# Moving the block epilogue of a selective-scan kernel from behind the sixth scan to behind the fourth

## Chip, cores and metric

The kernel runs on all 8 cores of one Trainium2 chip. Each core takes two of the 16 sequences; the cores exchange nothing. The metric is the device time in microseconds of the slowest core.

## What is computed

One layer: a layer norm of x, a state-space branch and a structured (tensor-train) linear branch, both added to x.

```python
x_and_res = x @ in_proj_w.T + in_proj_b
x_in = silu(x_and_res[..., :d_model]);  res = x_and_res[..., d_model:]
ssm = x_in @ x_proj_w.T + x_proj_b          # dlt_raw (16), Bm (1024), Cm (1024)
delta = clip(softplus(dlt_raw @ dt_proj_w.T + dt_proj_b), 1e-05, 0.1)
def step(h, inp):                           # h: d_model x 16 states
    dt, Bt, Ct, xt = inp
    dA = clip(exp(A * dt[..., None]), 1e-06, 1.0)
    h = clip(h * dA + (Bt * dt * xt)[..., None], -100.0, 100.0)
    y = sum(h, axis=-1) * Ct + D_param * xt
    return (h, y)
return y * silu(res) @ out_proj_w.T + out_proj_b
```

x is 16 x 2048 x 1024 in float32. The last line is y times silu(res), projected by the output weights.

## The kernel before

**Tiles.** A core's two sequences are cut into 8 chunks of 512 time steps (4 chunks each). The 1024 channels are 8 blocks of 128 partitions, and each channel has 16 states, so the recurrence of one chunk is 8 x 16 = 128 scans of 128 x 512. I write s(k,n) for the scan of block k, state n.

**The scan pipeline.** ACT computes `da` = exp(delta * A) for each scan (`emit_da`, L895) into a ring of 8 buffers; it may write the buffer of scan G only when scan G-8 is done. DVE runs the scan itself (L835) into `h_buf`, a ring of 8 slices (`HR = 8`); it may write slice G only when PE has consumed slice G-8. PE adds the 16 states of a block by a multiplication with the identity, accumulating in a PSUM bank (`emit_sigma`, L557; banks pS and pS2 alternate by block). I call this the sum of s(k,n). After every fourth scan a small DVE instruction (L845, "clip") saves the carries. When the 16 sums of block k are in, DVE's epilogue of that block (`emit_epi`) multiplies the bank by C (L806, writes y_s) and adds D*x (L814, writes y2_s); then POOL multiplies y2_s by silu(res) (L454) into the tile that the output projection reads.

```python
wt(v, "t", ("summ", cS * 128 + kk * NST + NST - 1))   # L806 waits: 16th sum
wt(v, "g", ("attn", cS * 8 + kk - 1))                 # L814 waits: POOL's L454 of the block before
if n == 5 and k >= 1:                                 # L851: where the epilogue of block k-1 stands
```

The epilogue of block k-1 thus stands in DVE's program inside block k. That of block 7 stands behind the last scan of the chunk. In chunk 0 those of blocks 0 and 1 stand together inside block 2.

**Three chunks at once.** While chunk c is scanned, the other engines also write out chunk c-1 (output projection and structured branch L585 and L590, evacuation L927, transposes L603, L936, residual addition on POOL L473 with its loads `xr_t`) and then prepare chunk c+1: layer norm of four tiles t = 0 to 3 (statistics on ACT L948 and L952, small mean and variance arithmetic on POOL L435, L437, L440, L443, L446, rstd on ACT L957 and L960, normalising on ACT, transposes on PE L624, evacuation L988 and L998), the input projection (16 groups, L647, evacuated with silu, L1020), the x projection (L682; L1033, L1039, L1045) and delta (L699, L1058, L1066, L1070).

**What sets the order.** Every engine runs one static list. PE's and ACT's lists are interleaved by a table `BNDS` of estimated times: before each group, `pump` and `apump` place the sums and `da` that the table finds due. For chunks 1 to 6 this puts the sums up to s(2,14) ahead of the fourth transpose group of the layer norm (t = 3), and the sums of s(2,15), s(3,0), s(3,1), s(3,2) right behind it, ahead of the input projection. POOL's list is sorted by due times too; in chunk 0 it holds `emit_w4`, which loads the structured weights with 16 DMAs of small pieces (L407), ahead of the first multiplication L454. ACT's exp/ln and its silu need different activation tables, so each switch costs an ACT_TABLE_LOAD.

Of the kernel before, what the change touches and what calls it, by code (L numbers as in the profile page):

```python
# [44 lines left out]
def build_core(M_in, M_out):  # L45
# [28 lines left out]
    with es:  # L74
# [79 lines left out]
        def mark(key, chain):  # L154
            M_out[key] = chain.n
# [5 lines left out]
        def wt(eng, chain_id, key):  # L161
            val = M_in.get(key, 0)
            if val > 0:
                wt_stat[0] += 1
                hk = (id(eng), chain_id)
                if wait_hi.get(hk, 0) >= val:
                    wt_stat[1] += 1
                    return
                wait_hi[hk] = val
                eng.wait_ge(CH[chain_id].sem, val)  # L170
# [31 lines left out]
        def h_sl(gn):  # L202
            r = gn % HR
            return h_buf[:, r * TC:(r + 1) * TC]
# [6 lines left out]
        def c_(tile, i):  # L211
            return tile[:, i:i + 1]
# [505 lines left out]
        def _(v):  # L718
            v_hi = [0]

            def vsw(val):
                if val > v_hi[0]:
                    v_hi[0] = val
                    v.wait_ge(VCH.sem, val)
# [35 lines left out]
            def emit_ffev4(q):  # L760
                for gidx in range(4 * q, 4 * q + 4):
                    half, m = divmod(gidx, 8)
                    if gidx == 8:
                        v.wait_ge(DS["pd2"], 16)
                    wt(v, "t", ("ffmm", gidx))
                    bank = [pO1, pO2][gidx % 2]
                    w4v = xr_t[0][:, :].bitcast(F16)
                    VCH(v.tensor_copy(w4v[:, m * 256:(m + 1) * 256],
                                      bank[:, 0:256]))
                    mark(("ffev", gidx), VCH)  # L770
                    if gidx in (7, 15):
                        mark(("w4ev", gidx // 8), VCH)

            def emit_wneg():
                v.wait_ge(DS["pd2"], 32 + 16 * 16)
                for kk in range(4):
                    VCH(v.tensor_scalar(w_ffn[4 + kk][:, 0:512],
                                        w_ffn[4 + kk][:, 0:512], -1.0, None,
                                        op0=ALU.mult))
                mark(("wneg",), VCH)  # L780
# [18 lines left out]
            def emit_epi(cS, kk, P):  # L799
                if cS == 0 and kk == 0:  # L800
                    wt(v, "t", ("ffmm", 15))
                wt(v, "t", ("summ", cS * 128 + kk * NST + NST - 1))
                sbank = [pS, pS2][kk % 2]
                if ep2_n[0] > 0:
                    vsw(ep2_n[0])
                ey = VCH(v.tensor_mul(y_s[:, :], sbank[:, :],  # L806
                                      Cf[P][kk][:, :]))
                mark(("epiy", cS * 8 + kk), VCH)
                if kk >= 1:
                    wt(v, "g", ("attn", cS * 8 + kk - 1))  # L810
                elif cS >= 1:
                    wt(v, "g", ("attn", (cS - 1) * 8 + 7))
                vsw(ey)
                ep2_n[0] = VCH(v.scalar_tensor_tensor(  # L814
                    y2_s[:, :], xin[P][kk][:, :], c_(d_cols, kk), y_s[:, :],
                    op0=ALU.mult, op1=ALU.add))
                mark(("epi2", cS * 8 + kk), VCH)

            for cS in range(nch):
                P = cS % 2  # L820
                b, ci = divmod(cS, NCHB)
                for k in range(DCH):
                    for n in range(NST):
                        gn = k * NST + n
                        G = cS * 128 + gn
                        wt(v, "a", ("da", G))
                        if G - HR >= 0:
                            wt(v, "t", ("summ", G - HR))
                            cn = clip_n.get((G - HR) // 4, 0)
                            if cn > 0:  # L830
                                vsw(cn)
                        if gn == 0 and last_clip[0] > 0:
                            vsw(last_clip[0])
                        init = 0.0 if ci == 0 else c_(carry[k], n)
                        s_n = VCH(v.tensor_tensor_scan(  # L835
                            h_sl(gn), da_r[gn % DAR][:, :], Bu[P][k][:, :],
                            init, op0=ALU.mult, op1=ALU.add))
                        mark(("scan", G), VCH)
                        if n % 4 == 3:
                            vsw(s_n)  # L840
                            base = (gn - 3) % HR
                            src = bass.AP(h_buf, base * TC + TC - 1,
                                          [[HR * TC, 128], [TC, 4]])
                            clip_n[(cS * 128 + gn - 3) // 4] = VCH(
                                v.tensor_scalar(carry[k][:, n - 3:n + 1], src,  # L845
                                                100.0, -100.0, op0=ALU.min,
                                                op1=ALU.max))
                        if cS == 0 and gn == 23:
                            for q_ in range(4):
                                emit_ffev4(q_)  # L850
                        if n == 5 and k >= 1:  # L851
                            if cS == 0 and k == 1:
                                pass
                            elif cS == 0 and k == 2:
                                emit_epi(0, 0, P)
                                emit_epi(0, 1, P)
                            else:
                                emit_epi(cS, k - 1, P)
                        if cS == 0 and gn == 96:
                            emit_wneg()  # L860
                emit_epi(cS, DCH - 1, P)
                last_clip[0] = clip_n.get((cS * 128 + 124) // 4, 0)
# [252 lines left out]
```

## Time and profile before

| | us |
|---|---|
| median of 2 runs | 2245.6 (2241.46 to 2249.75) |
| the profiled execution | 2249.66 |
| span of its slowest core (core 2) | 2247.9 |
| spans of the eight cores | 2225.2 to 2247.9 |
| mean granted TensorE clock, core 2 | 0.756 |
| first scan starts, core 2 | 301.7 |
| chain that ended last | PE 37%, DVE 21%, issue 12%, ACT 11%, DMA 9%, POOL 7% |

The span runs from the first to the last instruction of the slowest core; the device time is 1.8 us more. All rows below are of core 2 of the profiled execution, in us from the start of its span. In the timeline views the columns are start, duration, engine, line, operation, out<-in, shape and the number of merged instructions; in brackets stands how long the engine was idle before, and what ended that.

### The profile page before, as it was taken

What the parts mean: (1) busy time and instruction counts of PE and PEld (TensorE: products, weight loads), DVE (VectorE), ACT (ScalarE), POOL (GpSimd) and SP (SyncE); (2) the same over time, 40 slices, a digit from 0 to 9 for tenths busy, and PEclk for the clock granted to TensorE, in tenths of its full rate; (3) what the DMA queues carried; (4) which work ended last, traced back from release to release, by engine and by line L of the source; (5) the groups of instructions that cost most, each with busy time, mean ns of one, the idle gap of its engine ahead of it and who ended that gap; (6) DMA issues with size and microseconds to landing.
All of it is one profiled execution on the core that took longest, in us unless ns stands there. A gap on an engine that the chain in (4) does not pass through costs nothing.

```text
span 2247.9 us, 21779 instructions; the slowest of 8 cores (2225.2 to 2247.9 us)
## 1 busy us (share of the span) xinstructions
PE 1240.8 (55%) x5104; PEld 511.8 (23%) x5104; DVE 1612.4 (72%) x1600; ACT 1253.0 (56%) x1873; POOL 614.6 (27%) x506
## 2 busy tenths in 40 slices
PE   1222846265464857385729572867277627755444
PEld 1111313021121313131314131323132213322012
DVE  1332044069985999499949995899589967999980
ACT  0004465476456955695559655965586558745531
POOL 0000041318122161307131713171317131523001
PEclk9999976676585968696859785978598758866557
DMA  5672322630011301240024003310332022202001
GB/s 142 190 183 71 114 75 36 66 63 25 1 66 66 113 19 44 77 126 19 29 85 124 27 10 103 100 52 10 103 90 61 10 103 81 71 1 75 1 10 65
DMA packets 106882, 151.92 MB, mean 68 GB/s; under 512 B 53232, under 2 KB 53240, under 8 KB 106760
## 3 DMA queue, kind: packets, MB, share of 16 engines
q1 hardware_dynamic: 97128, 120.10, 18.3%
q0 software_dynamic: 6176, 19.93, 4.1%
q10 hardware_dynamic: 3456, 10.52, 1.5%
q8 instruction: 46, 0.75, 0.1%
q14 instruction: 76, 0.62, 0.1%
HBM read 124.26 MB, written 26.25 MB: 67 GB/s over the span
## 4 chain that ended last, share of the span: by engine, by line
PE 37%; DVE 21%; issue 12%; ACT 11%; DMA 9%; POOL 7%; SPq 1%; DVEq 0%; ACTq 0%; POOLq 0%
DVE h_buf L835 19%; PE pM L682 7%; PE pS L557 7%; PE pO L585 5%; DMA xr_t<-x 5%; PE pM L647 5%; PE pO L590 4%; PE pO L647 4%; POOL out_tm L473 3%; ACT da L895 3%; PE pO L682 2%; ACT rx L952 1%; ACT rx L948 1%; POOL wf L407 1%; PE pT L519 1%
## 5 line engine op out<-in xcount | busy, mean ns | idle before, releaser
L835 DVE TENSOR_TENSOR_SCAN h_buf<-da,cr,Bu 128x512 f16<-128x512 f16 x768 | 1053.3, 1427 | 114.1 <-PE pS L557 112.2
L895 ACT ACTIVATE da<-dlt,ac 128x512 f16<-128x512 f16 x1024 | 695.2, 715 | 292.3 <-DVE h_buf L835 290.4
L557 PE MATMUL pS<-h_buf,eye 128*128 128x512 f16 x1024 | 422.0, 475 | 332.4 <-DVE h_buf L835 322.6
L835 DVE TENSOR_TENSOR_SCAN h_buf<-da,Bu 128x512 f16<-128x512 f16 x256 | 331.8, 1351 | 157.5 <-ACT da L895 114.3
L454 POOL TENSOR_TENSOR Bu<-y_s,sres 128x512 f16<-128x512 f32 x64 | 126.2, 1973 | 763.4 <-DVE y_s L814 763.4
L557 PEld LDWEIGHTS pS<-h_buf,eye 128*128 128x128 f16 x1024 | 108.4, 107 | 569.9 <-issue 508.2
L682 PE MATMUL pM<-xin,rx 128*128 128x512 f16 (+1 forms) x832 | 197.2, 382 | 26.0 <-ACT sres L1020 22.0
L473 POOL TENSOR_TENSOR out_tm<-otm,xr_t 128x1024 f32<-128x1024 f16 x32 | 75.6, 2362 | 230.9 <-ACT otm L936 121.7
L647 PE MATMUL pM<-xnf,rin 128*128 128x512 f16 x512 | 133.1, 409 | 3.8 <-ACT sres L1020 2.5
L585 PE MATMUL pO<-Bu,wo 128*128 128x512 f16 x512 | 132.5, 406 | 3.1 <-POOL Bu L454 3.1
L647 PE MATMUL pO<-xnf,rin 128*128 128x512 f16 x512 | 123.6, 387 | 7.7 <-DMA rin<-wt_in 7.7
L590 PE MATMUL pO<-xnf,wf 128*128 128x512 f16 x512 | 123.2, 384 | 0.0
L519 PE MATMUL pT<-eye,rx 128*128 128x128 f16 x320 | 40.5, 307 | 140.6 <-DVE rx L732 140.6
L682 PEld LDWEIGHTS pM<-xin,rx 128*128 128x128 f16 (+1 forms) x832 | 79.7, 97 | 128.8 <-issue 36.6
L435 POOL TENSOR_SCALAR mcol<-sumx 128x1 f32<-128x1 f32 x32 | 12.6, 393 | 350.0 <-ACT rx L952 350.0
L876 ACT ACT_TABLE_LOAD x1 | 1.3, 1283 | 187.7 <-DVE rx L732 187.7
L624 PE MATMUL pT<-eye,xn_tm 128*128 128x128 f16 x128 | 16.2, 306 | 156.1 <-ACT xn_tm L967 94.2
L814 DVE SCALAR_TENSOR_TENSOR y_s<-xin,d_cols,y_s 128x512 f32<-128x512 f16 x64 | 56.2, 878 | 63.7 <-POOL Bu L454 57.1
L936 ACT ACTIVATE otm<-pTo 128x1024 f16<-128x1024 f16 x32 | 32.6, 1019 | 116.6 <-POOL out_tm L473 115.7
L927 ACT ACTIVATE ao<-pO,bcomb 128x512 f16<-128x512 f32 x64 | 43.8, 684 | 90.2 <-PE pO L590 90.1
L845 DVE TENSOR_SCALAR cr<-h_buf 128x4 f16<-128x4 f16 x256 | 72.6, 283 | 27.2
L624 PE MATMUL pT<-eye,xin 128*128 128x128 f16 x128 | 16.2, 307 | 136.6 <-ACT xnf L988 136.6
(83 smaller groups left out, 1539.3 us busy)
## 6 DMA issues: line engine op xcount, KB each, us to landing
rin<-wt_in SPq DMA_DIRECT2D x128, 256.0 KB, 2.8
rx<-wt_x SPq DMA_DIRECT2D x128, 256.0 KB, 2.7
x_t<-x SPq DMA_DIRECT2D x32, 512.0 KB, 4.6
xr_t<-x POOLq DMA_DIRECT2D x32, 512.0 KB, 5.0
y<-out_tm SPq DMA_DIRECT2D x32, 512.0 KB, 3.6
wt_in<-rin SPq DMA_DIRECT2D x16, 256.0 KB, 2.8
wt_x<-rin SPq DMA_DIRECT2D x16, 224.0 KB, 3.6
x_t<-w_in ACTq DMA_DIRECT2D x4, 512.0 KB, 3.9
```

The costliest lines, as they stand in the source:

```text
L454: GCH(gp.tensor_mul(Bu[P][k][:, :], y2_s[:, :], sres[P][k][:, :]))
L473: GCH(gp.tensor_add(out_tm[g % 2][:, :], otm16[:, :], xr_t[g % 2][:, :]))
L519: TCH(te.transpose(pT1[:, k * 128:(k + 1) * 128], wst16[j % 2][:, k * 128:(k + 1) * 128], eye16[:, :]))
L557: TCH(te.matmul(sbank[:, :], eye16[:, :], h_sl(gn), start=(n == 0), stop=(n == NST - 1)))
L585: TCH(te.matmul(bank[:, :], w_out[k][:, m * 128:(m + 1) * 128], Bu[P][k][:, :], start=(k == 0), stop=False))
L590: TCH(te.matmul(bank[:, :], w_ffn[k][:, m * 128:(m + 1) * 128], xn_f[P][:, k * TC:(k + 1) * TC], start=False, stop=(k == DCH - 1)))
L647: TCH(te.matmul(bank[:, :], rin[slot][:, k * 128:(k + 1) * 128], xn_f[P][:, k * TC:(k + 1) * TC], start=(k == 0), stop=(k == DCH - 1)))
L682: TCH(te.matmul(out_ap, rx[slot][:, k * ncols:(k + 1) * ncols], xin[P][k][:, :], start=(k == 0), stop=(k == DCH - 1)))
L814: ep2_n[0] = VCH(v.scalar_tensor_tensor(y2_s[:, :], xin[P][kk][:, :], c_(d_cols, kk), y_s[:, :], op0=ALU.mult, op1=ALU.add))
L835: s_n = VCH(v.tensor_tensor_scan(h_sl(gn), da_r[gn % DAR][:, :], Bu[P][k][:, :], init, op0=ALU.mult, op1=ALU.add))
L845: v.tensor_scalar(carry[k][:, n - 3:n + 1], src, 100.0, -100.0, op0=ALU.min, op1=ALU.max))
L895: ACH(sc.activation(da_r[gn % DAR][:, :], dlt[Ps][k][:, :], AF.Exp, scale=c_(a_cols[k], n)))
```

## The change

One number changes: the epilogue of block k-1 is issued when n == 3 instead of n == 5.

```diff
-                        if n == 5 and k >= 1:
+                        if n == 3 and k >= 1:
                             if cS == 0 and k == 1:
                                 pass
                             elif cS == 0 and k == 2:
                                 emit_epi(0, 0, P)
                                 emit_epi(0, 1, P)
                             else:
                                 emit_epi(cS, k - 1, P)
```

No other engine's list changes: PE, ACT, POOL and SP run the same instructions in the same order. On DVE 56 of the 64 epilogues move ahead of two scans, at 55 places (blocks 1 to 7 of 8 chunks; chunk 0 has none in block 1 and two in block 2).

The first place is DVE in chunk 0, inside block 2 (Bu_2 is the scan input of block 2, Cf_0 and Cf_1 the C tiles of blocks 0 and 1):

```order
 L835 SCALAR_TENSOR_TENSOR h_buf<-da,Bu_2 128x512 x4
 L845 TENSOR_SCALAR cr<-h_buf 128x4
-L835 SCALAR_TENSOR_TENSOR h_buf<-da,Bu_2 128x512 x2
 L806 TENSOR_TENSOR y_s<-pS,Cf_0 128x512
 L814 SCALAR_TENSOR_TENSOR y_s<-xin_0,d_cols,y_s 128x512
 L806 TENSOR_TENSOR y_s<-pS,Cf_1 128x512
 L814 SCALAR_TENSOR_TENSOR y_s<-xin_1,d_cols,y_s 128x512
-L835 SCALAR_TENSOR_TENSOR h_buf<-da,Bu_2 128x512 x2
-L845 TENSOR_SCALAR cr<-h_buf 128x4
 L835 SCALAR_TENSOR_TENSOR h_buf<-da,Bu_2 128x512 x4
```

The scans s(2,4) and s(2,5) stood ahead of the two epilogues and now stand behind them.

The second place is DVE in chunk 1, inside block 3 (Cf_2 belongs to block 2). Before:

```order
L845 TENSOR_SCALAR cr<-h_buf 128x4
L835 SCALAR_TENSOR_TENSOR h_buf<-da,cr,Bu_3 128x512 x2
L806 TENSOR_TENSOR y_s<-pS,Cf_2 128x512
L814 SCALAR_TENSOR_TENSOR y_s<-xin_2,d_cols,y_s 128x512
L835 SCALAR_TENSOR_TENSOR h_buf<-da,cr,Bu_3 128x512 x2
```

and of the changed kernel at the same place:

```order
L845 TENSOR_SCALAR cr<-h_buf 128x4
L806 TENSOR_TENSOR y_s<-pS,Cf_2 128x512
L814 SCALAR_TENSOR_TENSOR y_s<-xin_2,d_cols,y_s 128x512
L835 SCALAR_TENSOR_TENSOR h_buf<-da,cr,Bu_3 128x512 x4
L845 TENSOR_SCALAR cr<-h_buf 128x4
```

The scans s(3,4) and s(3,5) now stand behind the epilogue of block 2, in one row with s(3,6) and s(3,7).

## Rows read from the trace of the kernel before

**Rows 1.** The page: its first line and its busy times.
```profile
span 2247.9 us, 21779 instructions; the slowest of 8 cores (2225.2 to 2247.9 us)
PE 1240.8 (55%) x5104; PEld 511.8 (23%) x5104; DVE 1612.4 (72%) x1600; ACT 1253.0 (56%) x1873; POOL 614.6 (27%) x506
```
**Rows 2.** View of line L806: what ended DVE's idle time before it (us, times).
```profile
  PE pS L557: 54.2, 16
```
**Rows 3.** Timeline of DVE, chunk 1, from the layer norm to the epilogue of block 2.
```profile
680.47 4.33 DVE L835 TENSOR_TENSOR_SCAN h_buf<-da,cr,Bu 128x512 f16<-128x512 f16 x2 [10.62 <-PE pS L557]
...
707.47 2.46 DVE L835 TENSOR_TENSOR_SCAN h_buf<-da,cr,Bu 128x512 f16<-128x512 f16 x2
716.86 0.69 DVE L806 TENSOR_TENSOR y_s<-pS,Cf 128x512 f32<-128x512 f32 x1 [6.93 <-PE pS L557]
718.33 3.31 DVE L835 TENSOR_TENSOR_SCAN h_buf<-da,cr,Bu 128x512 f16<-128x512 f16 x2
```
**Rows 4.** DVE busy in the stretches behind block 2's epilogue, chunks 1 to 6.
```profile
717.00:839.00 122.00, 118.75 (x105) 0.81 0.24 70
...
sum 728.00, DVE 707.88; mean DVE 117.98
```
**Rows 5.** Timeline of PE, chunk 1: sums of s(2,15) and s(3,0) to s(3,2).
```profile
716.17 1.86 PE L557 MATMUL pS<-h_buf,eye 128*128 128x512 f16 x4 [1.37 <-ACT xnf L998]
```
**Rows 6.** Timeline of ACT, chunk 1, from the layer norm into the input projection.
```profile
710.01 0.29 ACT L957 ACTIVATE rstd<-vcol,eps_c 128x1 f32<-128x1 f32 x1 [2.85 <-POOL vcol L443]
...
721.73 0.72 ACT L895 ACTIVATE da<-dlt,ac 128x512 f16<-128x512 f16 x1 [1.31 <-DVE h_buf L835]
...
725.82 0.69 ACT L1020 ACTIVATE xin<-pO,bin_c 128x512 f16<-128x512 f32 x1 [0.80 <-PE pO L647]
727.98 0.69 ACT L1020 ACTIVATE xin<-pO,bin_c 128x512 f16<-128x512 f32 x1 [1.47 <-PE pO L647]
```
**Rows 7.** Timeline of POOL, chunk 1: residual additions, variance arithmetic of tiles 0 and 3.
```profile
653.50 2.72 POOL L473 TENSOR_TENSOR out_tm<-otm,xr_t 128x1024 f32<-128x1024 f16 x1 [12.64 <-ACT otm L936]
661.71 2.12 POOL L473 TENSOR_TENSOR out_tm<-otm,xr_t 128x1024 f32<-128x1024 f16 x1 [4.95 <-DMA xr_t<-x]
...
675.70 0.19 POOL L440 TENSOR_TENSOR nmr<-mcol 128x1 f32<-128x1 f32 x1
676.04 0.19 POOL L443 TENSOR_TENSOR vcol<-vcol,nmr 128x1 f32<-128x1 f32 x1
...
707.68 1.06 POOL L440 TENSOR_TENSOR nmr<-mcol 128x1 f32<-128x1 f32 x1
708.88 1.03 POOL L443 TENSOR_TENSOR vcol<-vcol,nmr 128x1 f32<-128x1 f32 x1
```
**Rows 8.** Timeline of DVE, chunk 0, around the epilogues of blocks 0, 1 and 2.
```profile
395.62 2.34 DVE L835 TENSOR_TENSOR_SCAN h_buf<-da,Bu 128x512 f16<-128x512 f16 x2 [2.53 <-ACT da L895]
...
459.32 0.75 DVE L814 SCALAR_TENSOR_TENSOR y_s<-xin,d_cols,y_s 128x512 f32<-128x512 f16 x1 [57.13 <-POOL Bu L454]
459.99 3.24 DVE L835 TENSOR_TENSOR_SCAN h_buf<-da,Bu 128x512 f16<-128x512 f16 x2
...
488.38 0.69 DVE L806 TENSOR_TENSOR y_s<-pS,Cf 128x512 f32<-128x512 f32 x1 [5.58 <-PE pS L557]
```
**Rows 9.** Timeline of POOL, chunk 0: the last of the 16 weight DMAs.
```profile
456.28 1.69 POOL L407 DMA_DIRECT2D wf<-w4r  x1 [9.98 <-issue]
```
**Rows 10.** Timeline of ACT, chunk 0, before and behind its wait of 44 us.
```profile
409.86 1.33 ACT L895 ACTIVATE da<-dlt,ac 128x512 f16<-128x512 f16 x2
...
416.54 0.69 ACT L1020 ACTIVATE sres<-pM,bin_c 128x512 f16<-128x512 f32 x1
461.29 1.28 ACT L895 ACT_TABLE_LOAD   x1 [44.06 <-DVE h_buf L835]
...
483.33 0.69 ACT L1020 ACTIVATE sres<-pO,bin_c 128x512 f16<-128x512 f32 x1
```
**Rows 11.** Timeline of PE, chunk 0: the first group of the x projection.
```profile
484.17 3.57 PE L682 MATMUL pM<-xin,rx 128*16 128x512 f16 x8 [9.96 <-ACT sres L1020]
```

## The prediction, made before the changed kernel ran

> **What bounds the kernel now.** The page comes first: DVE is the busiest engine with 72% of the span, yet 28% of its time is idle [rows 1]. So I asked where it idles, chunk by chunk, and whether the moved instruction stands at one of those places. The view of line L806 answers the second: only 16 of the 64 epilogues wait for PE, 54.2 us in all [rows 2]. The timeline shows the big ones. In chunk 1 the epilogue of block 2 waits 6.93 us [rows 3]; chunks 2 to 6 have the same wait at the same epilogue, about 7 us each. Chunk 7, which prepares no further chunk, has none. The 16 are those six, two in chunk 0, and a short one at the end of each of the eight chunks, which doesn't move.
>
> The last sum of block 2 is held by the layer norm of the next chunk: PE runs it only at 716.17, released by ACT's evacuation L998 [rows 5], and ACT's tile-3 work had started with a wait of 2.85 us for POOL's variance [rows 6]. So up to 716.86 a chunk is paced by ACT, POOL and PE in turns. From there on it is DVE's: of the 122 us behind that epilogue it is busy 118.75, and of all six stretches 707.88 of 728 [rows 4]. The idle 3.25 us are spread over the hand-overs between its 105 instructions. The next chunk's first sum and first `da` wait for DVE's first scan, so a delay of DVE at the end of a chunk moves the whole next chunk.
>
> **The change, part by part. (a) Two scans fall behind the wait: loss.** In chunk 1 the scans s(3,4) and s(3,5) ran at 707.47, in time that would have been idle anyway [rows 3]. Now DVE meets the epilogue at 707.5 and waits until the last sum. The two scans follow, when DVE is the bound. They took 2.46 us as a row and the next instruction followed 2.4 us after their start. POOL's multiplication, which stretches the two scans behind an epilogue to 3.31 us, stretches two scans in either order, so that cancels. The cost is +2.4 us a chunk, 6 chunks: +14.2 us (chunk 4 has no carry operand and slightly shorter scans). ACT gets two `da` buffers later too. It stands at 721.73 waiting for DVE already, and then idles 0.80 and 1.47 us for PE [rows 6], which takes up most of 2.4 us. The lead of PE over DVE behind 717 shrinks, but DVE's pauses are not PE's.
>
> **(b) POOL is left alone in its variance arithmetic: gain.** While those two scans ran, POOL did L440 and L443 of tile 3, and they took 1.06 and 1.03 us. The same instructions for tile 0, at 675.7, took 0.19 each [rows 7], and DVE then idled (10.62 us before 680.47) [rows 3]. In the changed kernel DVE is idle at 707.7, so both should take 0.19: 0.87 + 0.84 = 1.71 us. That arithmetic is on the chain to the sum (POOL, ACT L957, the normalising, PE's transposes, L998, the sum), as ACT waited for exactly this [rows 6], so the epilogue's wait ends 1.7 us sooner: 6 x 1.7 = -10.3 us. Its bounds are 0 and -1.71 a chunk. I take the full value, because all six chunks show the same pair of durations under the same pair of scans.
>
> This is what the Trainium skill states (SBUF — State Buffer, "Who interferes with whom"): DVE and GpSimd share a port pair, and a DVE instruction with two SBUF inputs contends with a GpSimd instruction that reads SBUF. The rows agree: 1.06 us beside a scan and 0.19 without. Without this rule (b) would be nothing and the sum 10 us higher.
>
> **(c) The epilogues that don't wait.** The 47 others merely change places with two scans on a saturated DVE: 0. In blocks 1 and 2 of a chunk the two scans come 1.5 us later than before; PE catches up with DVE a few sums later anyway. The residual additions on POOL take 2.12 us when they get there first and 2.72 beside scans [rows 7]; which is which may change at one of four tiles, and that chain is critical. Bounds -0.9 to +0.9 us a chunk, taken as 0.
>
> **(d) The long stop in chunk 0.** The second L814 of the pair waits 57.13 us for POOL [rows 8], whose sixteen weight DMAs end at 456.28 + 1.69 [rows 9]. That end is POOL's own, so it stays. But s(2,4) and s(2,5), which ran at 395.62 ahead of the stop [rows 8], now come after it. ACT's `da` s(2,12) needs the buffer of s(2,4). Before, ACT got past that one, through two silu and one more `da`, until 416.54 + 0.69 = 417.23. Now it stops where the second of the pair of 409.86 would start, 409.86 + 1.33 - 0.72 = 410.47 (a single `da` takes 0.72) [rows 6, 10]. So 6.7 us of ACT's work slides behind the stop. It resumes after the first scan at 461.29, the same time as before, for that scan then was the one that it waited for. Behind the stop ACT is the bound: it has no pause up to the silu at 483.33 [rows 10], for which PE waited 9.96 us [rows 11], and the last sum of block 2 stands right behind that PE group. So the wait of DVE at 488.38 [rows 8] ends 6.7 us later: +6.7. PE has one projection group more to redo there, 1.9 to 3.6 us, inside its 9.96 us of waiting.
>
> The Trainium skill (ScalarE: Activation LUTs, "What ACT_TABLE_LOAD costs") adds a drain of about 1.38 us to each load of 1.28. The trace disagrees: the load of 461.29 is followed by work at 462.58, and in the 6.7 us that slide stand four loads which leave no room for it. With the drain (d) would be 5.5 us more.
>
> At the block-2 epilogue of chunk 0 part (a) holds once more: two scans without carry, 2.34 us as a row [rows 8], so +2.3. No variance arithmetic runs there, so (b) gives nothing back. Chunk 0 costs 9.0 us.
>
> **Sum.** 14.2 - 10.3 + 9.0 = +12.9 us. On the profiled execution's own 2249.66 (span 2247.9 and 1.8 around it) that is 2262.5. The median of the runs shown stands 4.1 us under it, so I predict 2245.6 + 12.9 = 2258.5 us, slower by 0.6%. About 2% is what a measurement of this kernel can tell from no change, so this counts as no change.
>
> **The rivals.** *A, POOL gives nothing back.* The layer-norm chain is held by something else, such as ACT's own `da` ahead of tile 3, and only the scans count: 14.2 + 9.0 = +23.2, 2268.8 us. Against it stands ACT's wait of 2.85 us for L443 [rows 6].
>
> *B, the stop in chunk 0 costs only its scans.* ACT makes up the 6.7 us. Then 3.9 + 2.3 = +6.2, 2251.8 us. For it: ACT has many later pauses in that chunk. Against: none before 483.33, where it matters.
>
> *C, not slower.* DVE regains the scans behind 717, and POOL's relief stays. The place is the stretch of rows 4. If DVE had to wait there for PE or ACT by more than 2.4 us in one piece, part (a) would be zero and each chunk would be 1.7 us shorter: -10.3 + 9.0 = -1.3, 2244.3 us; with chunk 0 absorbed too, -10.3, 2235.3 us. It decides from the point where a pause over 2.4 us stands behind the block-2 epilogue. All the idle time there is 3.25 us in 122, over 105 instructions, and the timeline marks no long piece in it.
>
> *D, more than priced.* The residual additions or other POOL work fall beside scans more often (+0.9 a chunk), or PE's smaller lead lets DVE wait (up to 1.3 us at the later epilogues): +13 on top, 2271 us.
>
> **How the numbers follow.** Forecast 0.55, A 0.12, B 0.13, C 0.10, D 0.10. The range 2247 to 2273 holds the forecast, A, B and D and leaves most of C and the rarest ends out; it also takes in that the two runs shown lie 8 us apart. Faster by over 2% would be under 2201, which no case reaches: 0.01. Slower by over 2% is over 2290, twice A's loss: 0.03. The rest, 0.96, is within 2%.
>
> **What would show it right or wrong.** In the profile after, the block-2 epilogue of chunks 1 to 6 should wait about 7.7 us (6.93 + 2.46 - 1.7) and start 1.7 us sooner after the chunk's first scan; L440 and L443 of tile 3 should take 0.19; scans s(3,4) and s(3,5) should be the stretched pair; each chunk should last 0.7 us longer. In chunk 0 ACT should wait about 51 us instead of 44, and DVE's L806 of block 2 should start at about 495 instead of 488.4. Long L440 in tile 3 would show A, a chunk 0 longer by 2 us B, chunks shorter than before C.

## The result and the profile after

The changed kernel takes 2255.97 us (median of 19 runs, 2247.81 to 2272.36), the kernel before 2247.11 us in 18 runs beside it. The ratio is 1.005, with a 95% interval of 1.0033 to 1.0067: slower by 11 us, give or take 4. The ratios here and below leave out executions in which the cores of a die show a lower granted clock and take longer; the medians don't, so the two can differ by some us. I had predicted 2258.5, 12.9 us over the median known then, in a range of 2247 to 2273. The profiled execution took 2257.06 us; its slowest core is core 5, and all rows of the kernel after are of that core.

The page, first line and busy times, answering to [rows 1]:

```profile
span 2255.3 us, 21671 instructions; the slowest of 8 cores (2238.1 to 2255.3 us)
PE 1246.4 (55%) x5104; PEld 508.9 (23%) x5104; DVE 1609.4 (71%) x1600; ACT 1254.1 (56%) x1873; POOL 601.8 (27%) x506
```

The view of line L806, what ended DVE's idle time before it (us, times), answering to [rows 2]:

```profile
  PE pS L557: 70.4, 16
```

DVE does the same work (1609 us against 1612) and waits more: still 16 epilogues, but 70.4 us instead of 54.2. These are two different cores. About 4.2 us of the difference are the six waits of chunks 1 to 6, 4.4 us the wait of block 2's epilogue in chunk 0 (5.58 to 9.95), and 7.7 us a wait of block 1's epilogue right ahead of the stop in chunk 0 (2.09 and 9.76). That last one differs from core to core (0 to 9.8 us in the kernel after) and costs nothing, as it lies inside a stop that ends when POOL is done.

DVE in chunk 1 around block 2's epilogue, answering to [rows 3]:

```profile
719.81 2.46 DVE L835 TENSOR_TENSOR_SCAN h_buf<-da,cr,Bu 128x512 f16<-128x512 f16 x2 [5.64 <-PE pS L557]
722.38 0.17 DVE L845 TENSOR_SCALAR cr<-h_buf 128x4 f16<-128x4 f16 x1
730.24 0.69 DVE L806 TENSOR_TENSOR y_s<-pS,Cf 128x512 f32<-128x512 f32 x1 [7.69 <-PE pS L557]
731.03 0.75 DVE L814 SCALAR_TENSOR_TENSOR y_s<-xin,d_cols,y_s 128x512 f32<-128x512 f16 x1
731.71 5.66 DVE L835 TENSOR_TENSOR_SCAN h_buf<-da,cr,Bu 128x512 f16<-128x512 f16 x4
```

The wait is 7.69 us, where 7.7 was worked out. From the clip of s(3,3) to the epilogue pass 7.7 us; before it was 9.4 (707.47 to 716.86), of which two scans used 2.4. The four scans behind it stand in one row with the stretch of one pair in it (5.66 = 3.31 + 2.35). The order change shows as step (a) said.

POOL's arithmetic of tile 3 in the same chunk, and ACT's first instruction behind it, answering to [rows 7] and [rows 6]:

```profile
722.77 0.19 POOL L440 TENSOR_TENSOR nmr<-mcol 128x1 f32<-128x1 f32 x1
723.10 0.19 POOL L443 TENSOR_TENSOR vcol<-vcol,nmr 128x1 f32<-128x1 f32 x1
...
723.39 0.29 ACT L957 ACTIVATE rstd<-vcol,eps_c 128x1 f32<-128x1 f32 x1 [1.15 <-POOL vcol L443]
```

1.06 and 1.03 us have become 0.19 and 0.19, and ACT's wait fell from 2.85 to 1.15 us, by 1.70. Step (b) had 1.71. In the kernel after both instructions take 0.19 to 0.20 us at tile 3 in all six chunks, on all eight cores.

Chunk 0, answering to [rows 8], [rows 10] and [rows 11]: DVE behind the stop and at block 2's epilogue, ACT's wait, PE's first x projection group.

```profile
465.39 0.75 DVE L814 SCALAR_TENSOR_TENSOR y_s<-xin,d_cols,y_s 128x512 f32<-128x512 f16 x1 [58.90 <-POOL Bu L454]
...
501.10 0.69 DVE L806 TENSOR_TENSOR y_s<-pS,Cf 128x512 f32<-128x512 f32 x1 [9.95 <-PE pS L557]
```
```profile
412.56 0.72 ACT L895 ACTIVATE da<-dlt,ac 128x512 f16<-128x512 f16 x1
467.37 0.72 ACT L895 ACTIVATE da<-dlt,ac 128x512 f16<-128x512 f16 x1 [54.09 <-DVE h_buf L835]
468.11 1.28 ACT L1020 ACT_TABLE_LOAD   x1
469.41 0.69 ACT L1020 ACTIVATE sres<-pM,bin_c 128x512 f16<-128x512 f32 x1
```
```profile
496.88 3.57 PE L682 MATMUL pM<-xin,rx 128*16 128x512 f16 x8 [9.76 <-ACT sres L1020]
```

ACT now stops behind a single `da`; the second `da` of that pair, two silu and one more `da` are left for the time behind the stop. Its wait of 54.09 us is that of core 5, the longest; the mean of the eight cores went from 42.0 to 48.7 us, +6.6. From the end of the stop to the epilogue pass 501.10 - 465.39 = 35.7 us, before 488.38 - 459.32 = 29.1: +6.6. PE's wait for ACT is as long as before, so PE's one extra group was hidden.

**The time by stretches.** A chunk splits at two instructions of DVE's timeline: its first scan and the L806 of block 2. These are means over the eight cores, in us, read from those start times. "c0 stop" ends at the second L814 of chunk 0.

```
                           before    after   change
ahead of the first scan    299.01   297.46    -1.54
c0 first scan to stop end  155.63   155.75    +0.12
c0 stop end to epilogue 2   28.90    35.56    +6.66
c0 behind epilogue 2       119.29   122.10    +2.81
c1-c6 to epilogue 2        651.19   642.01    -9.18
c1-c6 behind epilogue 2    731.40   741.35    +9.95
c7, both stretches         188.96   188.95     0.00
behind the last epilogue    63.76    63.80    +0.04
span                      2238.13  2246.97    +8.84
```

Chunks 1 to 6 together cost 0.8 us. Nearly the whole loss, 9.5 us, is chunk 0. The first row varies from core to core by 17 us before and isn't touched by the change. In the profiled execution of the kernel before it is the longest of all: the experiments below have 293.5 to 296.8 us there. So the stretches are compared, and not the whole spans.

### The profile page after: what moved, and what is told of

It is laid out like the page before. It is cut to its first block, busy times and chain, and to the rows that moved or that the text cites. A ratio compares the mean times of both kernels' runs of the same rounds, so it can differ in the third digit from the quotient of the medians.

```text
span 2255.3 us, 21671 instructions; the slowest of 8 cores (2238.1 to 2255.3 us)
## 1 busy us (share of the span) xinstructions
PE 1246.4 (55%) x5104; PEld 508.9 (23%) x5104; DVE 1609.4 (71%) x1600; ACT 1254.1 (56%) x1873; POOL 601.8 (27%) x506
## 4 chain that ended last, share of the span: by engine, by line
PE 33%; DVE 25%; issue 13%; ACT 12%; DMA 9%; POOL 6%; SPq 1%; DVEq 0%; ACTq 0%; POOLq 0%
DVE h_buf L835 22%; PE pS L557 6%; PE pM L682 6%; PE pO L585 5%; DMA xr_t<-x 4%; PE pO L590 4%; PE pM L647 4%; POOL out_tm L473 3%; ACT da L895 3%; PE pO L647 3%; PE pO L682 3%; ACT rx L952 1%; ACT rx L948 1%; POOL wf L407 1%; PE pT L519 1%
## 5 line engine op out<-in xcount | busy, mean ns | idle before, releaser
L835 DVE TENSOR_TENSOR_SCAN h_buf<-da,Bu 128x512 f16<-128x512 f16 x256 | 336.4, 1373 | 153.2 <-ACT da L895 114.3
L435 POOL TENSOR_SCALAR mcol<-sumx 128x1 f32<-128x1 f32 x32 | 12.6, 392 | 351.8 <-ACT rx L952 351.8
L814 DVE SCALAR_TENSOR_TENSOR y_s<-xin,d_cols,y_s 128x512 f32<-128x512 f16 x64 | 50.2, 785 | 65.8 <-POOL Bu L454 58.9
L806 DVE TENSOR_TENSOR y_s<-pS,Cf 128x512 f32<-128x512 f32 x64 | 44.1, 689 | 70.4 <-PE pS L557 70.4
```

What stands on the lines that cost most here:

```text
L814: ep2_n[0] = VCH(v.scalar_tensor_tensor(y2_s[:, :], xin[P][kk][:, :], c_(d_cols, kk), y_s[:, :], op0=ALU.mult, op1=ALU.add))
L835: s_n = VCH(v.tensor_tensor_scan(h_sl(gn), da_r[gn % DAR][:, :], Bu[P][k][:, :], init, op0=ALU.mult, op1=ALU.add))
```

## The experiments

The first five edits are shown against the changed kernel. Stretches are again means over eight cores of the profiled execution. The chip's own spread makes the times good to a few us only; the stretches are good to some tenths.

### Chunk 0 alone, and all but chunk 0

```diff
-                        if n == 3 and k >= 1:
+                        if n == (3 if cS == 0 else 5) and k >= 1:
```

> Epilogue behind n == 3 in chunk 0 only, behind n == 5 in the rest. Theory (the stop in chunk 0 carries the loss): end of the stop to block 2's epilogue 35.6 us instead of 28.9, behind it 122.1 instead of 119.3, chunks 1 to 7 as before; total +9.5 us, which is the whole loss. Rival (the loss is spread over the chunks): chunk 0 the same, but the total under +3 us because later chunks win it back.

```diff
-                        if n == 3 and k >= 1:
+                        if n == (5 if cS == 0 else 3) and k >= 1:
```

> Epilogue behind n == 3 in chunks 1 to 7 only. Theory: chunk 0 as before (28.9 and 119.3 us); in chunks 1 to 6 the way to block 2's epilogue 1.5 us shorter, the way behind it 1.6 us longer; total +0 to +2 us, not to be told from 0. Rival (forecast as written: scans +14.2, POOL -10.3): +3.9 us.

Chunk 0 alone: ratio 1.0053 (1.0031 to 1.0074), the whole loss. Stop end to epilogue 35.53 us, behind it 122.08; chunks 1 to 6 took 1381.9 us against 1382.6. All but chunk 0: 1.0014 (0.9995 to 1.0032), with 28.94 and 119.28 in chunk 0 and 1383.4 us in chunks 1 to 6. The rival of the first run falls by its time, 12 us where under 3 were due. That of the second (+3.9 us) can't be told by the time, whose interval reaches from -1 to +7 us; it falls by the stretches, +0.8 us in chunks 1 to 6. The loss is chunk 0's, and the rest is an exchange of nearly equal parts.

### The pair of epilogues at the stop

```diff
-                        if n == 3 and k >= 1:
+                        if n == (5 if cS == 0 and k == 2 else 3) and k >= 1:
```

> Changed kernel, except that the pair of epilogues in block 2 of chunk 0 stays behind n == 5. Theory: s(2,4) and s(2,5) run before the stop again, ACT's wait is 44 us again, and end of the stop to block 2's epilogue goes back from 35.6 to 28.9 us; the stretch behind it stays at 122.1. Total 6.7 us under the changed kernel, about +2 us against before. Rival (6.7 us come from elsewhere in the chunk, for instance s(3,4) and s(3,5)): it stays at 35.6.

Stop end to epilogue 28.94 us, behind it 122.03; ratio 1.0018 (0.9986 to 1.005). ACT's wait in this kernel:

```profile
455.67 1.28 ACT L895 ACT_TABLE_LOAD   x1 [44.55 <-DVE h_buf L835]
```

It waits again at a table load and for 44 us, as in [rows 10]. So the 6.7 us hang on the place of the two scans s(2,4) and s(2,5). What stays, 2.8 us behind the epilogue, is the other pair, s(3,4) and s(3,5), priced at 2.3.

### Block 2's epilogue alone in chunks 1 to 6

```diff
-                        if n == 3 and k >= 1:
+                        if n == (3 if 1 <= cS <= 6 and k == 3 else 5) and k >= 1:
```

> Only the epilogue of block 2 in chunks 1 to 6 moves behind n == 3; all others stay. By steps (a) and (b) of the prediction: way to this epilogue -1.7 us, way behind it +2.4 us per chunk, total +3.9. If the way behind it is only 1.5 us longer as in the changed kernel, the shortfall of 0.9 us belongs to this site; if it is 2.4, it belongs to the later epilogues (blocks 3 to 6), which meet POOL's delta work at another place. L440 and L443 of tile 3 at 0.19 in either case.

Way to the epilogue -9.6 us over the six chunks, way behind it +14.0; ratio 1.0034 (1.001 to 1.0058). Steps (a) and (b) had +14.2 and -10.3 for exactly this. So the shortfall of the changed kernel (+9.95 instead of +14.2) is not in them. It comes with the other epilogues, which the prediction had put at nothing.

### The later epilogues alone

```diff
-                        if n == 3 and k >= 1:
+                        if n == (3 if 1 <= cS <= 6 and k >= 4 else 5) and k >= 1:
```

> Epilogue behind n == 3 only from block 4 on (epilogues of blocks 3 to 6) in chunks 1 to 6, all others behind n == 5. Theory (the 0.9 us that step (a) lacked belong to these epilogues, which meet POOL's delta work at another place): way to block 2's epilogue as before (108.7 us), way behind it 0.9 us shorter, 121.6 instead of 122.5; total -5 us. Rival (as the prediction's step (c) had it): no change.

A mixed result: way behind the epilogue -0.5 to -0.7 us in five chunks, 3.1 us together of the 4 that were missing, and +3.0 in chunk 4, so 0 in sum; ratio 0.999 (0.995 to 1.0031). On the slowest core, in chunk 4, the epilogue of block 4 shows:

```profile
1445.43 0.69 DVE L806 TENSOR_TENSOR y_s<-pS,Cf 128x512 f32<-128x512 f32 x1 [3.48 <-PE pS L557]
```

There the earlier epilogue meets a sum that isn't done. It waits 0.9 to 3.5 us in chunk 4 on all eight cores, and up to 2.3 us on single cores in other chunks. In the changed kernel no epilogue of blocks 3 to 6 waits; that fits with the two scans of step (a), which have made DVE later against PE. The gain of 0.6 in the other chunks is busy time, not waits: behind block 2's epilogue the durations of DVE's 105 instructions add up to 124.7 us before and 123.9 with the later epilogues alone. The same shows in the changed kernel: on core 0 in chunk 1, the DVE instructions behind the epilogue take 124.7 us in sum before and 126.4 after, with two scans of 2.5 us more among them, so all were stretched by 0.8 us less. It is POOL's delta work (L480 to L500) that runs beside them. L806 is never stretched (0.66 to 0.69 us in all 64 of each core, before and after), which may be why: moved to another place, it covers another piece of POOL's work. That last link is argued, not shown.

### The layer norm's arithmetic on ACT

```diff
-                        wt(sc, "g", ("lnv", g))
-                        l0 = ACH(sc.activation(c_(rstd, t), c_(vcol, t), AF.Ln,
-                                               bias=eps_c[:, :]))
+                        m1 = ACH(sc.activation(c_(mcol, t), c_(sumx, t),
+                                               AF.Identity, scale=-1.0 / D))
...
+                        m2_ = ACH(sc.activation(c_(vcol, t), c_(mcol, t),
+                                                AF.Square))
...
+                        m3 = ACH(sc.activation(c_(vcol, t), c_(vcol, t),
+                                               AF.Identity, scale=-1.0,
+                                               bias=eps_c[:, :]))
...
+                        l0 = ACH(sc.activation(c_(rstd, t), c_(sumsq, t), AF.Ln,
+                                               scale=1.0 / D, bias=c_(vcol, t)))
...
-                        wt(sc, "g", ("nm", g))
+                        l2 = ACH(sc.activation(c_(nmr, t), c_(mcol, t),
+                                               AF.Identity, scale=c_(rstd, t)))
```

POOL's "ln" events do nothing here; each ACT instruction waits for the one before.

> Kernel before (n == 5) with the layer norm's small arithmetic on ACT instead of POOL (six single-column instructions of 0.29 us with 0.1 us between them, 2.3 us per tile, in place of 2.7 + 1.2 us with two hand-overs to POOL). No port is shared with DVE, so tiles 1 to 3 get 1.6 us shorter each and tile 0 stays: -4.8 us per chunk, chunks 0 to 6 about -29 us in all. Rival (the chain is held elsewhere, as by the transposes or by da): under 5 us gained.

With n == 5: 2185.55 us, ratio 0.9733 (0.9713 to 0.9754). The gain is 59 us, twice what was expected: the way to the epilogue is 8.3 us shorter per chunk on average, not 4.8, and chunk 0 is shorter by another 7 us. Tile 3 in chunk 1 on ACT:

```profile
690.60 0.18 ACT L941 ACTIVATE mcol<-sumx 128x1 f32<-128x1 f32 x1
690.87 0.20 ACT L944 ACTIVATE vcol<-mcol 128x1 f32<-128x1 f32 x1
691.17 0.29 ACT L947 ACTIVATE vcol<-vcol,eps_c 128x1 f32<-128x1 f32 x1
691.55 0.29 ACT L951 ACTIVATE rstd<-sumsq,vcol 128x1 f32<-128x1 f32 x1
691.94 0.29 ACT L954 ACTIVATE rstd<-rstd,mhalf_c 128x1 f32<-128x1 f32 x1
692.33 0.29 ACT L958 ACTIVATE nmr<-mcol,rstd 128x1 f32<-128x1 f32 x1
```

From the first of them to the end of the last pass 2.0 us. Part of what I had missed stands in the kernel before, in POOL's timeline ahead of tile 1:

```profile
681.58 2.13 POOL L473 TENSOR_TENSOR out_tm<-otm,xr_t 128x1024 f32<-128x1024 f16 x1 [3.31 <-DMA xr_t<-x]
683.68 2.06 POOL L454 TENSOR_TENSOR Bu<-y_s,sres 128x512 f16<-128x512 f32 x1
685.72 0.22 POOL L435 TENSOR_SCALAR mcol<-sumx 128x1 f32<-128x1 f32 x1
```

The arithmetic was queued behind a residual addition and an epilogue's multiplication, and ACT waited 4.45 us for it. In the four tiles of that chunk ACT's waits for L443 are 1.2, 4.5, 2.8 and 2.9 us, where 1.2 is the undisturbed one. POOL's L435 and L437 are stretched beside scans too (0.84 and 1.21 us at tile 2, 0.23 and 0.20 at tile 0).

> Changed kernel (n == 3) with the same arithmetic on ACT. This takes away what step (b) gives back, as there is no POOL arithmetic beside the two scans. Theory: against e5_ln5 it loses step (a) whole and chunk 0: 1.5 to 2.4 us per chunk with the way to block 2's epilogue equal, plus 9.5, so +18 to +23 us. Rival (step (b) isn't POOL's relief, the shorter way has another cause such as the earlier epilogues): the same +9 us as between the changed kernel and before.

With n == 3: 2208.91 us, 0.9843 (0.9819 to 0.9866), 23 us over its partner. The way to the epilogue is +0.5 us per chunk (it was -1.5), the way behind +1.7 as before, chunk 0 +6.6 and +2.3 at its two places. The rival falls: without POOL in the chain, step (b) gives nothing. The epilogue of block 2, chunk 1, in this kernel:

```profile
711.75 0.69 DVE L791 TENSOR_TENSOR y_s<-pS,Cf 128x512 f32<-128x512 f32 x1 [7.36 <-PE pS L542]
```

The wait grew from 4.90 to 7.36, by the full 2.46 us of the pair, instead of the 0.76 by which it grew with POOL in the chain (6.93 to 7.69). The difference is 1.70.

### The weight DMAs in four groups

```diff
-                for kk in range(4):
+                emit_w4l(0)
+
+            def emit_w4l(kk):
                     for (src, dstk, colb) in (("r", kk, 0), ("i", kk, 512),
...
                     ev.append((18.5, "w4", 0))
+                    for kk in (1, 2, 3):
+                        ev.append(((16 * kk + 2) * SCAN_NS + 0.5 + 2.7, "w4l", kk))
```

> Kernel before (n == 5) with POOL's sixteen weight DMAs in four groups: four ahead of its first multiplication, four behind each of the first three. The stop of 57 us ends when the first four are issued, at about 404 instead of 459. Theory: DVE, ACT and PE were all idle in the stop, so 45 to 55 us go. Rival (the input projection, its loads or the later DMA groups take the place of the stop): under 20 us.

With n == 5: 2213.7 us, 0.9856 (0.9833 to 0.9878), 31 us gained and less than expected. The stop is gone:

```profile
398.36 1.17 POOL L460 TENSOR_TENSOR Bu<-y_s,sres 128x512 f16<-128x512 f32 x1
```
```profile
399.70 0.75 DVE L820 SCALAR_TENSOR_TENSOR y_s<-xin,d_cols,y_s 128x512 f32<-128x512 f16 x1 [0.31 <-POOL Bu L460]
...
469.44 1.22 DVE L841 TENSOR_TENSOR_SCAN h_buf<-da,Bu 128x512 f16<-128x512 f16 x1 [11.15 <-PE pS L563]
```

First scan to the second L814 takes 101.2 us instead of 155.6, so 54.4 us went. The way from there to epilogue 2 is 12.6 us longer (41.45) and the one behind it 8.5 us longer (127.83, with 14.2 us of idle DVE instead of 3.5): the second row shows one of the new waits, 11.15 us for PE. So 21 of the 54 us came back as a longer way behind. That the other engines had got ahead of DVE at the beginning of the stop, and no longer are, fits but wasn't followed engine by engine. The rival was right in part.

> Changed kernel (n == 3) with the same four groups. Theory: without the long stop no work of ACT can slide behind it, so the loss in chunk 0 falls from 9.5 to 2 to 4 us, and against e7_split5 this is +1 to +5 us. Rival (the 6.7 us are ACT's with or without the stop): +9 us.

With n == 3: 2217.2 us, 0.9875 (0.9853 to 0.9897). Chunk 0 takes 271.7 us against 270.5, +1.2, where the same move cost 9.6 with the stop in place. The cores of either kernel spread over 8 to 9 us in this chunk, so +1.2 says only that little is left. The 6.7 us are no price of the earlier epilogue as such, but of what is caught behind a long stop.

### One scan later instead of two earlier

Against the kernel before:

```diff
-                        if n == 5 and k >= 1:
+                        if n == (6 if 1 <= cS <= 6 and k == 3 else 5) and k >= 1:
```

> The epilogue of block 2 in chunks 1 to 6 goes the other way, behind n == 6, so that a third scan runs in the time in which DVE waits. Theory: the wait before it falls from 6.94 to 5.7 us, the way behind it is 1.2 us shorter, total -7 us, less up to 0.9 us per chunk if the third scan runs beside POOL's L446 on the way to the sum. Rival (the order beyond n == 5 doesn't matter, as the lead of PE is then used up): 0.

2235.56 us, ratio 0.9951 (0.9923 to 0.9978): 11 us faster than before. DVE on its slowest core, chunk 1:

```profile
709.17 3.64 DVE L835 TENSOR_TENSOR_SCAN h_buf<-da,cr,Bu 128x512 f16<-128x512 f16 x3
718.61 0.69 DVE L806 TENSOR_TENSOR y_s<-pS,Cf 128x512 f32<-128x512 f32 x1 [5.80 <-PE pS L557]
719.41 0.75 DVE L814 SCALAR_TENSOR_TENSOR y_s<-xin,d_cols,y_s 128x512 f32<-128x512 f16 x1
720.08 1.28 DVE L835 TENSOR_TENSOR_SCAN h_buf<-da,cr,Bu 128x512 f16<-128x512 f16 x1
721.46 0.87 DVE L845 TENSOR_SCALAR cr<-h_buf 128x4 f16<-128x4 f16 x1
```

Three scans run in the dead time, the wait is 5.8 us in four chunks, close to the 5.7 expected (6.9 in chunk 4 and 6.2 in chunk 5), and the way behind is 2.0 us shorter per chunk on average (12.2 in six), not 1.2. Part of the surplus is in these rows: POOL's multiplication now meets the clip, which it stretches by 0.70 us (0.17 to 0.87), instead of a scan, which it stretches by 0.85 (the pair 2.46 to 3.31). The remainder lies further on and I haven't traced it; it is busy time too, as DVE is busy there for some 2.5 us less in chunks 1, 2, 3 and 6 (116.7 to 116.8 us instead of 119.3 to 119.4) and idle for about as long as before. The way to the epilogue became longer in chunks 4 to 6 (+1.1, +0.4, +0.6).

### Both aids, and an epilogue placed block by block

> Kernel before (n == 5) with both aids: the layer norm's arithmetic on ACT (measured alone -59 us) and the weight DMAs in four groups (alone -31 us). Theory: they touch different stretches and add up, about 2155 us. Rival: in chunk 0 they meet, and 10 us or more are lost.

With both aids and n == 5: 2152.29 us, ratio 0.956 (0.9492 to 0.9628). The two aids add up, as expected: 59 + 31 = 90, measured 95 under the kernel before beside it, though the interval is wide (84 to 114 us). The stretches agree: chunk 0 is 39.8 us shorter, with 6.3 and 33.3 for the aids alone, and the ways to the epilogue in chunks 1 to 6 are 48.4 us shorter, with 50.0 and 0.8.

The placement block by block, against the kernel with both aids:

```diff
-                        if n == 5 and k >= 1:
+                        if n == (6 if k == 3 and cS < 7 else 3 if 1 <= cS <= 6 and k >= 4 else 5) and k >= 1:
```

> As e11_both5, with the epilogue placed block by block: behind n == 6 in block 3 of chunks 0 to 6, behind n == 3 from block 4 on in chunks 1 to 6, else behind n == 5. Theory: -1.2 us at block 3 and -0.9 us behind it per chunk, -10 to -14 us against e11_both5. Rival: the two gains do not add, under 4 us.

2151.49 us, 0.9567 (0.9525 to 0.9608): no difference to be told from its partner, where 10 to 14 us less were expected. The stretches behind block 2's epilogue are 0.6 to 1.4 us shorter in five chunks and 1.0 us longer in chunk 4. The epilogue of block 4 now waits for PE (on core 0 for 0.9 us in chunks 1, 2, 3 and 5); in chunk 4 of the slowest core:

```profile
1371.86 0.69 DVE L797 TENSOR_TENSOR y_s<-pS,Cf 128x512 f32<-128x512 f32 x1 [1.47 <-PE pS L548]
```

DVE is earlier there than PE's sums, and the gains don't add, much as the rival had it. The version with n == 6 at block 3 alone, on top of both aids, wasn't tried.

## Why the prediction held

**(a) The two scans behind the wait, +14.2 us.** Right. Alone it measured +14.0 (block 2's epilogue alone), and the arithmetic of the wait, 6.93 + 2.46 - 1.7, came out at 7.69.

**(b) POOL left alone, -10.3 us.** Right. 1.70 us per chunk at ACT's wait, -9.6 and -9.2 us on the way to the epilogue in two kernels, and nothing without POOL in the chain. Rival A falls with the kernel that has the arithmetic on ACT. One reading was wrong: not all six chunks had the same pair of durations. In chunk 4 it was L437 and L440 that were stretched (1.10 and 1.13 us) and L443 took 0.19; ACT's wait fell there by as much, from 2.95 to 1.13 us.

**(c) The other epilogues, 0.** Wrong as a size: -4.1 us (9.95 - 14.0), by some 0.7 us per chunk. The bounds had been set for the residual additions only. I had not looked at the delta work of POOL, which runs beside DVE for some forty us of a chunk (773 to 815 on core 0 in chunk 1 before). Scans take up to 2.1 us there instead of 1.26, and the clip 0.87 instead of 0.17. The residual additions did change: on core 2 the second of each chunk takes 2.5 to 3.0 us in all six, where it took 2.1 in three; on core 5 it stays at 2.1 to 2.3. This may be part of the few tenths by which the way to the epilogue shortened less than 1.7.

**(d) The stop in chunk 0, +6.7 and +2.3 us.** Right: +6.66 and +2.81. Rival B falls, as it said that ACT makes it up. The point that decided was that ACT has no pause between the stop and the silu for which PE waits. One detail was miscounted: the work that slid holds three table loads, not four (468.11, 470.11 and 472.14 in the kernel after). Three loads of 1.28, two `da` of 0.72 and two silu of 0.69 make 6.66 us, the measured amount. There is no room in it for the drain that the prediction speaks of, and the 5.5 us that it gives for one count a load too many.

**Rival C** needed a pause of over 2.4 us behind epilogue 2. There is none; DVE's idle time there stays at 3.2 to 3.5 us in both kernels, as a mean over the cores. **Rival D** didn't come either, but its mechanism exists: block 4's epilogue in chunk 4, with the later epilogues alone, waits 3.48 us.

The sum was 12.9 us with 8.8 measured in the spans and 11 in the ratio. The difference to the spans, 4.1, is (c) with 4.1 and a stretch ahead of the first scan that was 1.5 us shorter by chance, less 1.5 of small differences in the other terms, above all (b), which gave 9.2 of its 10.3. The median after, 2255.97 us, lies 2.5 us under the forecast, but the step from before to after, 8.9 us by the medians, lies 4.0 under the sum. The 1.5 us between these two are luck: the kernel before came out at 2247.11 us and not at the 2245.6 from which the forecast was counted.

Of the signs that were named, the wait of 7.7 us, the 0.19 us and the stretched pair came as written. ACT's wait in chunk 0 grew by 6.6 us where 7 was written (51 against 44). Block 2's epilogue there came at 501.10 on core 5 and not at 495, since the stop on that core ended at 465.39 and not at 459.32; counted from the stop it is 6.7 us later. The way to the epilogue of chunks 1 to 6 became 1.5 us shorter, not 1.7. One sign failed: a chunk became 0.1 us longer and not 0.7, which is (c) again.

Chunk 0 keeps the loss, while in chunks 1 to 6 a loss of 10 and a gain of 9 meet.

## What to carry to other kernels

Where an instruction waits in an in-order queue, what stands right ahead of it runs for nothing and what stands right behind it is paid for; so a move is worth its independent work at the few places with a wait, and little elsewhere (here 0.7 us per chunk, from other instructions being stretched). Look also at what the idle engine no longer disturbs: here 1.7 of 2.4 us per chunk came back since single-column arithmetic on POOL ran without DVE beside it. And where one long stop freezes several engines, ask how far each of them gets before it, since the work that is caught behind can cost more than the instructions that were moved (here 6.7 us for two scans of 2.3).

## What the runs showed that I had not expected

Six dependent single-column instructions on ACT take 2.0 us, while POOL with two hand-overs took 4.1 us for the same result at tile 3 (L952's end at 707.2 to L974 at 711.22), and more where its queue held other work. Most of that difference is stretch: with DVE idle the way over POOL took 2.4 us in the kernel after (722.24 to 724.60). Moving them brought 59 us of 2245, the largest single gain of the study, from instructions of 0.2 to 0.3 us.

DVE's clip of 4 columns takes 0.17 us alone and 0.87 us beside a POOL multiplication: 0.7 us lost on an instruction that does almost nothing. A pair of scans of 2.46 us loses 0.85 to the same multiplication, so here the loss hardly depends on how long the stretched instruction is.

A stop of 57 us in one chunk was worth only 31 when it went. The way to its end became 54 us shorter, and the rest of the chunk 21 us longer.
